# Gated cross attention with a routed expert layer: the probabilities made in turned form by a second pass of the scores

## The reference

```python
def xattn(q, k, v, ...):                      # q = layernorm(x), k = v = ctx_1024
    qh, kh, vh = heads(q @ wq.T + bq), heads(k @ wk.T + bk), heads(v @ wv.T + bv)
    logits = einsum('bhqd,bhkd->bhqk', qh, kh) / sqrt(16) + causal_mask     # -1e9 above the diagonal
    out = einsum('bhqk,bhkd->bhqd', softmax(logits), vh)
    return merge_heads(out) @ dense_w.T + dense_b
def ffn(h, router_w, w1, b1, w2, b2):         # h = layernorm(x), 4096 rows
    logits = h @ router_w                                                   # 14 experts
    e = argmax(logits); weight = softmax(logits)[e]
    return (gelu(h @ w1[e] + b1[e]) @ w2[e] + b2[e]) * weight
x = x + tanh(g_xattn) * xattn(layernorm(x), ctx, ctx, ...)
x = x + tanh(g_ffn) * ffn(layernorm(x), ...)
```

## Time and profile before

| what | value |
|---|---|
| time, median of 3 runs | 466.85 us (466.75 to 467.65) |
| span of the profiled execution | 479.0 us |
| PE busy | 453.8 us (95%) |
| PEld busy | 371.5 us (78%) |
| DVE busy | 350.8 us (73%) |
| ACT busy | 314.3 us (66%) |
| POOL busy | 303.2 us (63%) |
| mean granted TensorE clock | 0.980 |

### The profile page before, as it was taken

How to read it: one execution, slowest core, us unless ns; L and a number is a source line. 1 busy time by engine, 2 the same in 40 slices (tenths; PEclk the granted TensorE clock), 3 DMA queues, 4 the chain that set the end, 5 groups by cost and what they waited for, 6 DMA issues and landing times.

```text
span 479.0 us, 16593 instructions
## 1 busy us (share of the span) xinstructions
PE 453.8 (95%) x4775; PEld 371.5 (78%) x4775; DVE 350.8 (73%) x1128; ACT 314.3 (66%) x1481; POOL 303.2 (63%) x668
## 2 busy tenths in 40 slices
PE   8999999999999999999999998959799999999991
PEld 4888888888888888888888887849699997545550
DVE  3668999899999999999999987645336443645640
ACT  2689999899899899898998997231222222344440
POOL 5476587687876877877868676566445555445321
PEclk9899999999999999999999999988989999999997
DMA  6274556211112112111120079795778887798500
GB/s 222 66 240 139 160 164 176 53 42 47 56 33 59 40 33 66 33 44 55 34 68 15 14 203 246 235 210 161 254 249 281 280 249 235 240 344 251 167 10 6
DMA packets 38765, 65.68 MB, mean 137 GB/s; under 512 B 12457, under 2 KB 27055, under 8 KB 38704
## 3 DMA queue, kind: packets, MB, share of 16 engines
q1 hardware_dynamic: 26272, 35.33, 25.3%
q10 hardware_dynamic: 7424, 19.60, 12.9%
q0 software_dynamic: 5008, 10.01, 7.6%
HBM read 55.84 MB, written 9.99 MB: 137 GB/s over the span
## 4 chain that ended last, share of the span: by engine, by line
PE 86%; DVE 4%; another core or an unknown queue 2%; issue 2%; DMA 2%; ACT 1%; SPq 1%; POOL 0%; POOLq 0%; DVEq 0%
PE bank L1566 11%; PE bank L1635 11%; PE bank L1474 9%; PE bank L1482 7%; PE bank L1625 7%; PE bank L1574 6%; PE bank L1558 6%; PE bank L1702 6%; PE bank L1517 5%; PE bank L1496 5%; PE bank L1615 2%; PE bank L1621 2%; PE bank L1553 2%; PE bank L1461 2%
## 5 line engine op out<-in xcount | busy, mean ns | idle before, releaser
L857 ACT ACTIVATE arena<-bank,negmax 128x128 f32<-128x128 f32 x512 | 179.6, 402 | 13.7 <-DVE negmax L1136 13.6
L857 ACT ACTIVATION_READ_ACCUMULATOR arena<-bank,negmax 128x1 f32 x512 | 123.6, 241 | 0.0
L1136 DVE TENSOR_REDUCE negmax<-bank 128x4 f32<-128x512 f32 x128 | 84.4, 681 | 12.5 <-PE bank L1558 12.2
L610 POOL DMA_INDIRECT out<-g_out,g_name x39 | 39.0, 1000 | 66.5 <-DVE g_name L1091 51.3
L1566 PE MATMUL bank<-C,arena 128*128 128x128 f32 x512 | 78.9, 276 | 0.1
L815 ACT ACTIVATE hid_t<-bank,w_ring 128x128 f32<-128x128 f32 x100 | 28.5, 370 | 70.3 <-PE bank L1474 44.5
L1566 PEld LDWEIGHTS bank<-C,arena 128*128 128x128 f32 x512 | 63.2, 142 | 9.1 <-ACT arena L857 0.8
L1635 PE MATMUL bank<-arena 128*128 128x128 f32 x512 | 68.1, 276 | 1.3 <-DMA arena<-ctxt 1.0
L1635 PEld LDWEIGHTS bank<-arena 128*128 128x128 f32 x512 | 62.2, 192 | 3.1 <-issue 2.4
L1474 PE MATMUL bank<-g_xt,w_ring 128*128 128x128 f32 x400 | 52.3, 287 | 8.1 <-DVE g_xt L1079 8.1
L1474 PEld LDWEIGHTS bank<-g_xt,w_ring 128*128 128x128 f32 x400 | 50.2, 202 | 9.7 <-issue 9.4
(11 more groups left out here) (179 smaller groups left out, 1000.7 us busy)
## 6 DMA issues: line engine op xcount, KB each, us to landing
...
```

The lines of the kernel that those rows point to most:

```text
L610: pool.indirect_dma_start(out=out_rows, out_offset=bass.IndirectOffsetOnAxis(ap=g_name[:, r, 0:1], axis=0), in_=g_out[:, r, :], in_offset= ...
L857: ins = act.activation(probs[:, q, v, :], bank[q][:, v * P:(v + 1) * P], ACT.Exp, bias=negmax[:, b.par, h:h + 1], accum_out=rsum[:, b.par, ...
L1136: dve.tensor_reduce(negmax[:, b.par, q * HQ:(q + 1) * HQ], bank[q][:, :].rearrange("p (v k) -> p v k", v=HQ), axis=AX_X, op=ALU.max, negat ...
```

## The change

The probabilities are no longer transposed. The scores are computed twice: first as before with queries on the partitions, only to find the row maxima; then with keys on the partitions (`key_scores`), so that the exponentials come out already turned, as `attend` wants them. A row maximum is now a value per column of the bank and can't be an activation's bias. It is added on TensorE instead: `split` (VectorE) cuts the negated maxima into three bfloat16 parts whose sum is the float32 value, `turn_maxima` turns all of them with one bfloat16 matmul, `turned_maxima` (ScalarE) copies them, and 16 bfloat16 matmuls with a one-hot selector (`chosen_bf`) add the parts to every key's row. `exponentials` are then four activations of 128 x 512 without bias or accumulator. The row sums come from columns of ones beside the values: `values` is preset to 1 and each head's 32 output rows hold 16 features and 16 copies of the sum. `keep_heads` (ScalarE) copies `attend`'s bank once whole and twice with a mask, `merge` (GpSimd) adds the two halves.

The division moves to DMAs: `move_sums` takes the sums (SBUF to SBUF) to 128 partitions x 16, `reciprocal` inverts them, `store_inverses` writes them to a table in DRAM, `spread_inverses` reads the table back, each row repeated over 16 partitions, and `normalise` multiplies one step later than before (batch u = t-5). Everything behind it moves a step back too. The router's share of x is now taken from x itself, loaded turned (`xt`, 512 KB for four batches), with 8 matmuls and one transpose for four batches. The masks come ready as bfloat16 from the host, the scaling of the queries moves from VectorE to ScalarE, and the loop has one step more; the last scores are inside it.

```diff
+            def split(b):
+                m = negmax[:, b.par, :].rearrange("p (q v) -> p q v", q=QUADS)
...
+                dve.tensor_copy(parts[:, :, 0, :], m).then_inc(split_step, 1)
+                dve.wait_ge(split_step, b.n * 3 + 1)
+                dve.tensor_tensor(rest, m, parts[:, :, 0, :], ALU.subtract).then_inc(split_step, 1)
+                dve.wait_ge(split_step, b.n * 3 + 2)
+                dve.tensor_copy(parts[:, :, 1, :], rest).then_inc(split_step, 1)
+                dve.wait_ge(split_step, b.n * 3 + 3)
+                dve.tensor_tensor(parts[:, :, 2, :], rest, parts[:, :, 1, :], ALU.subtract).then_inc(max_split, 1)
...
-            def exponentials(b, q):
...
-                for v in range(HQ):
-                    h = q * HQ + v
-                    ins = act.activation(probs[:, q, v, :], bank[q][:, v * P:(v + 1) * P], ACT.Exp,
-                                         bias=negmax[:, b.par, h:h + 1], accum_out=rsum[:, b.par, h:h + 1])
+            def exponentials(c):
+                act.wait_ge(key_scores_ready, c.n + 1)
+                wait(act, av_done, c.n)
+                for q in range(QUADS):
+                    act.activation(probs_t[:, q, :, :].rearrange("p v s -> p (v s)"), bank[4 + q][:, :],
+                                   ACT.Exp).then_inc(probs_ready, 1)
+            def keep_heads(c, at=bank[6]):
+                act.wait_ge(av_done, c.n + 1)
+                wait(act, sums_moved, c.n * 32)
+                act.activation(with_sums.rearrange("p e n -> p (e n)"), at[:, :], ACT.Copy).then_inc(sums_kept, 1)
+                wait(act, merged_ready, c.n)
+                for e_ in range(HT):
+                    ins = act.activation(head_rows[:, e_, :], at[:, e_ * D:(e_ + 1) * D], ACT.Copy,
+                                         scale=const("headmask")[:, e_:e_ + 1])
+                ins.then_inc(halves_kept, 1)
...
-            def transpose_probs(b, q):
-                for v in range(HQ):
-                    pe.wait_ge(probs_ready, b.n * H + q * HQ + v + 1)
-                    ins = pe.transpose(bank[4 + q % 2][:, v * P:(v + 1) * P], probs[:, q, v, :], ident)
+            def key_scores(b):
+                for g in range(P // RT):
+                    for q in range(QUADS):
+                        rt = slice(RT * q, RT * q + RT)
+                        pe.matmul(bank[4 + q][:, :].rearrange("p (v q) -> p v q", v=HQ)[:, :, g * RT:(g + 1) * RT],
+                                  keys_of_bf[rt, g, :], later_key_bf[rt, :, :], start=(g == 0), stop=False)
+                for v in range(HQ):
+                    for q in range(QUADS):
+                        rt = slice(RT * q, RT * q + RT)
+                        pe.matmul(bank[4 + q][:, v * P:(v + 1) * P], k_masked[rt, b.par, v // HT, v % HT, :],
+                                  q_t[rt, b.par, v // HT, :], start=False, stop=False)
+                pe.wait_ge(max_turned_ready, b.n + 1)
+                for v in range(HQ):
+                    for q in range(QUADS):
+                        rt = slice(RT * q, RT * q + RT)
+                        ins = pe.matmul(bank[4 + q][:, v * P:(v + 1) * P],
+                                        chosen_bf[rt, v:v + 1].to_broadcast([RT, P]), max_turned[rt, :],
+                                        start=False, stop=(v == HQ - 1))
+                ins.then_inc(key_scores_ready, 1)
...
+            def move_sums(c):
+                hold(sums_kept, c.n + 1)
+                hold(inverses_ready, c.n)
+                sp.dma_start(sums[0:P // 2, :], with_sums[DH:P:VB, 0, :]).then_inc(sums_moved, 16)
+                sp.dma_start(sums[P // 2:P, :], with_sums[0:P:VB, 1, :]).then_inc(sums_moved, 16)
+            def store_inverses(c):
+                hold(inverses_ready, c.n + 1)
+                hold(inverses_spread, c.n * 16)
+                for e_ in range(HT):
+                    sp.dma_start(inverse_rows_of[e_:H // HT:HT, :],
+                                 inverses[e_ * P // 2:(e_ + 1) * P // 2, :]).then_inc(inverses_stored, 16)
+            def spread_inverses(c):
+                hold(inverses_stored, c.n * 32 + 32)
+                hold(attn_ready, c.n)
+                sp.dma_start(inverse_wide, inverse_rows_of.rearrange("r (o n) -> r o n", o=1)
+                             .to_broadcast([H // HT, DH, D])).then_inc(inverses_spread, 16)
...
+            def normalise(u):
+                dve.wait_ge(inverses_spread, u.n * 16 + 16)
+                dve.wait_ge(merged_ready, u.n + 1)
+                wait(dve, dense_done, u.n)
+                dve.tensor_tensor(attn_t, merged, inverse_wide, ALU.mult).then_inc(attn_ready, 1)
```

833 lines of the change are left out of this document (440 added, 393 removed).

## The result

The changed kernel takes 512.82 us (511.45 to 519.78, 4 runs) against 466.82 us (466.75 to 467.65, 4 runs) of the kernel before on the same chip: a ratio of 1.0967, 95% interval 1.0941 to 1.0993. It is 46 us slower; 460 was predicted, with 443 to 482 as the range. Of the cases told ahead, rival 1 (the inverse ring decides) has the right sign and its upper end of 503 comes nearest, but in the quiet steps the landing of the store, on which that rival rested, is not what was mis-sized. The profiles of experiments 7, 9 and 13 come from the slowest of their four executions (523.51, 528.51 and 506.85 us), so the step times read from them lie somewhat above those of the medians.

What follows compares the result with a forecast made beforehand. TensorE's issue was taken to bound the attention phase, other engines hidden. 30 steps x 8.20 = 246, plus 9 for the queue, gave 255 against 261.6: -6.6 us, so 460.2, say 460 us; range 443 to 482.

Steps and rivals of the forecast that it cites:

- rival 1: Attention steps: inverse ring decides, small store to DRAM landing in 3.0 to 3.9 us; 477 to 503 us; chance 0.27.
- TensorE's step: TensorE's issue per attention step: 8.72 less 2.30 removed plus 1.78 added, 8.20 us (8.1 to 8.6).
- Rival 3: TensorE doesn't gain: weight loads not hidden behind 128-column matmuls, step of 8.6, 12 us more, 472; chance 0.05.
- First ring and ScalarE: Maxima, split and turn just hidden behind TensorE's other work (split by 0.3 us); ScalarE some 6.5 us a step, no bound.
- Second ring: Inverses through DMAs, one `normalise` to the next: 3.65 plus two landings, 8.05 us, under TensorE's 8.20.
- Lw: Landing of the inverses' store of 64-byte pieces to DRAM: 2.3 us taken, bounds 1.86 and 3.9; called the likeliest error.
- Lr: Landing of the spread that reads the inverses' table and writes 128 KB: 2.1 us.
- sums' side branch: Move of the sums lands at 7.3 us in the step, `reciprocal` reached at some 7.5: hidden by 0.2.
- Big loads: SyncE's queue: small DMAs stand behind W2 and `xt` loads; 5.4 plus 3.5, together 9 us (0 to 18).
- the term for `xt`: Sums land up to 1.2 us late behind the load of `xt`; 0.5 for 7 steps, 3.5 us.
- The ends: First step and hand-written end of the attention phase: gains and losses taken as 0, with 4 us either way.
- the queue's 9: Total delay of the small DMAs behind big loads in SyncE's queue: 9 us (0 to 18).

Runs made afterwards that it cites:

- experiment 7: Changed kernel with the 14 W2 loads issued in SyncE's steps 28 to 34 instead of 5 to 11: 517.68 us, ratio 1.1019.
- 9: Changed kernel with the move of the sums issued by ScalarE right behind its copy instead of by SyncE: 524.78 us.
- 13: Changed kernel, all DMAs kept, division left out: `normalise` multiplies by ones, `reciprocal` takes ones, neither waits on the ring's DMAs: 501.57 us, ratio 1.0669.
- experiment 2: Changed kernel without the division: no move of sums, `reciprocal`, stores or spread, `normalise` multiplies by ones: 479.65 us, ratio 1.0237.
- 6: Changed kernel with the move of the sums issued ahead of the loads of x, ctxt and xt on SyncE: 533.39 us, ratio 1.1341.
- experiment 14: Changed kernel with `reciprocal` taken of ones without waiting for the sums, `normalise` still waiting for the spread, division left out: 544.60 us, ratio 1.1628.
- 4: Changed kernel with `attend` and its copy ahead of the keys, and `reciprocal` ahead of residual and statistics: 529.92 us, ratio 1.1304.
- 11: Changed kernel with the sums moved by four DMAs of half the rows instead of two, all on SyncE: 537.36 us, ratio 1.1464.
- 10: Changed kernel with the sums' move issued by ScalarE behind its copy and `reciprocal` ahead of the two statistics: 520.29 us, ratio 1.1069.
- 3: Changed kernel with the 14 W2 loads issued by ScalarE, SyncE issuing everything else: 519.58 us, ratio 1.1076.
- experiment 12: Kernel before, with the first two gathers of expert rows issued behind GpSimd's last attention step instead of mid-step: 476.83 us, ratio 1.0148.
- 17: Changed kernel, division left out, no VectorE wait for sums or spread, loads of x, ctxt and xt cut to 32 columns: 493.51 us, ratio 1.0518.
- 16: Changed kernel with loads of x, ctxt and xt cut to 32 columns from the fifth batch on: 512.81 us, ratio 1.0881.
- 5: Changed kernel with all ring DMAs kept, but `normalise` multiplies by ones without waiting for the spread: 524.51 us, ratio 1.1196.

## Why the prediction was wrong, step by step

**TensorE's step: right within its bounds.** 8.20 us (8.1 to 8.6) were forecast, 8.51 is the quiet step without a ring. The large parts agree: the second scores 0.95 (1.10; 219.54 to 220.49 in the timeline below), the second mask 0.23, the maxima's parts 0.22. (The mean of all 30 is 8.47, so the loop is 254.2 us and not 246: 8 us.) The ordinary steps without a ring are 8.06 and 8.15 long, but of every four one takes 8.65 and one 9.32. The router's share of x was nearly right: 0.57 us in one step of four and a transpose of 0.15 in the next, 0.18 a step for 0.15. What was too low is, first, the projections, which start 0.97 to 1.00 apart where the earlier trace rows gave 0.87 and 0.90. Second, in the step of 9.32 the next mask starts 0.89 us after the maxima's parts and not 0.22, at a turn of the loop; TensorE waits there for nothing that the profile shows, and the cause stays open. Rival 3 is out: with 32 loads the second scores take 0.95, the first with 16 take 1.01 (212.02 to 213.03).

```profile
219.31 0.40 PE L1655 MATMUL bank<-C 32*128 32x128 bf16 x16
219.54 1.11 PE L1660 MATMUL bank<-arena 32*128 32x128 f32 x32
220.49 0.39 PE L1666 MATMUL bank<-max_turned,C 32*128 32x128 bf16 x16
```

**First ring and ScalarE: right.** Without the second ring TensorE is busy 192.73 of 195.72 us in the quiet steps, so maxima, split and turn are hidden all but 0.13 us a step; ScalarE is at 65% there.

**Second ring, the inverses: the step that failed.** The prediction made it 8.05 us, "under TensorE's 8.20", and so free. As a sum of parts it was short by 0.56. In the round shown above, from `normalise` to the first store it is 3.40 us for 3.1; from the first store to the second 0.64 for 0.33, since the ring's stores take 0.53 to 0.62 us each to issue and not the 0.33 of the earlier trace rows; from the second to the spread 1.90 for Lw's 2.3 (2.1 on average); from the spread to `normalise` 2.67 for Lr's 2.1. The wakes, 0.2 in the sum, are inside these. So Lr, the spread's landing, was mis-sized most, and Lw, named as the likeliest error, was too high if anything. By these sizes alone, with nothing else wrong, the step is 8.61 for 8.20, 12 us in 30 steps, and the forecast 472. The 2.0 us that the Trainium skill gives as the fixed cost of one DMA (DMA: Bandwidth & Descriptors, Anatomy of one DMA, which is about DMAs issued by GpSimd) fit the store in a quiet queue, 1.9; for the spread's 128 KB its fit, 2.0 us and the bytes by 436 GB/s, gives an estimate of 2.3, and the trace has 2.67. The larger error is in the form: it gave each landing one value and closed the ring through VectorE alone. The ring as it is costs 33.2 us (2). The runs show that the landing of a 4 KB store goes from 1.8 to over 5 us with what is still landing from other DMAs (6, 13 and 14; 6 us behind W2), and that SyncE's order of stores, spread, loads and moves closes paths of its own: over the sums' move behind `load_x` (4), over two more issues (11), and over the table and ScalarE's copy (13).

**The sums' side branch: wrong.** "Hidden by 0.2" became a wait in 5 of the 23 quiet steps (2.9 us), since the move stood 0.8 us on average behind the copy. In three of the five, with 2.4 of the 2.9 us, the load of `xt` had been issued ahead of the move; so much came true of the term for `xt`, 3.5 us in the forecast. Mending the branch alone gained nothing (6, 9, 10).

**Big loads: wrong in size.** 9 us were forecast with 18 as the bound. W2's stretch alone lost 17.6 against the kernel without a ring (76.06 and 58.46), and experiment 7 moves 10.2 of it away with W2. In three of the seven steps a pair delays the stores by 2.4 to 4.1 us, not by up to 1.6, and the clock then adds a part that the forecast did not have. That it is the same by either queue (3: 75.95 for 76.06) is what a rule of the Trainium skill would have said (DMA: Bandwidth & Descriptors, Queues, rings and completion order): the semaphore's write of a DMA lands only after every earlier write of that DMA engine, across its queues. The trace of experiment 14 fits it too: the stores' last two writes come 0.5 and 0.6 us after the last one of a scatter that another engine had issued before them. Over fifteen kernels with the ring, of 133 pairs of stores that landed more than 2.2 us after the second issue, 116 had a scatter of names or a store of token rows ahead of them that was still landing 1.2 us after that issue; of the 197 quicker ones 52 had.

**The ends: wrong.** "I take 0, with 4 either way" became 3.8 us at the start and 12.6 at the end, both seen without a ring and read from one profile of each kernel. (The start varies: the second scores of the kernel before are at 22.54 and 24.50 in its two profiles and at 23.73 in experiment 12, so that 1.8 to 3.8 us are the change's.) The end is in the main the depth of the new pipeline: rows are stored a step later against the last scores, so the first gather is 9.5 us later. Experiment 12 moves the gather alone, by 7.5 us, and loses 6.8 in the end; what the other 5.8 are is not shown. At the start the first step with masks and second scores comes behind waits for the router and the split, and TensorE is at 1.2 GHz behind them (granted clock 0.50 from 24.0 to 26.1, second scores 2.03 us), as the timeline without a ring shows:

```profile
23.04 0.69 PE L1761 MATMUL bank<-C,arena 128*128 128x128 f32 x2 [1.53 <-DVE arena L1237]
23.66 0.61 PE L1636 MATMUL bank<-C 32*128 32x128 bf16 x16
24.06 2.03 PE L1641 MATMUL bank<-arena 32*128 32x128 f32 x32
```

**The account.** From 468.4 us: TensorE's saving -6.4, start +3.8, end +12.6 (together 10.0 of spans, 11.2 of medians: 479.65, shown by experiment 2). The ring adds 33.2. Against the forecast of 460 that is 8 us for TensorE's step, 16 for the ends and 24 for the ring (33 where the queue's 9 stood); the other 4 are the base (468.4 for 466.85) and the difference between spans and medians. The ring's 33.2 can be walked up in steps: its DMAs with small loads and no wait on VectorE, 13.9 (to 493.5); the loads' full bytes, 8.1 (to 501.6); VectorE's two waits, 11.2 (to 512.8). But these are no prices of causes. The two kernels between leave the division out and have the slower scatter, and about half of the 13.9 lies behind the loop (17). Taken in another order the numbers change: with the waits in place the bytes cost nothing (16), and one wait fewer goes with 32 us more (14).

**What stays open.** Why the scatter of names lands a microsecond later in the kernels that do not divide, and so how much of experiments 5, 13, 14 and 17 is the edited wait and how much that scatter. A kernel that divides and then scatters to other places, or one with another engine's scatter moved away from the stores, would tell; neither was run. Nor was a double table of inverses, or the batch's `dense` one step later, tried.
